# A perceiver block on one core: token groups cut as 2, 4, 4, 4, 2 batches in place of 4, 4, 4, 4

## What is computed

```python
x = x + cross_attention(_layernorm(x), ctx)      # q, k, v.reshape(B, -1, 16, 64): 16 heads over pairs of rows, softmax
x = x + selective_scan_block(_layernorm(x))      # 1024 channels, 16 states
x = x + moe_ffn(_layernorm(x))                   # 16 experts, the best 4 of a token, 512 -> 256 -> 512
```

```python
x_inner = x @ x_proj_w.T;  xc = silu(causal_conv4(x_inner) + conv_b)
B = x @ B_proj_w.T;  C = x @ C_proj_w.T
delta = softplus(x @ dt_proj_w.T + dt_proj_b);  A = -exp(A_log)
h = exp(delta * A) * h + delta * B * xc          # a recurrence over the 64 tokens of a batch
y = sum_s(h * C) + D * xc;  out = y @ out_proj_w.T
```

## Time and profile before

| | |
|---|---|
| median of 3 runs | 1436.08 us (1433.49 to 1438.27) |
| profiled execution | 1434.95 us, its span 1432.4 us |
| TensorE busy | 1084.5 us (76%) |
| VectorE busy | 990.2 us (69%) |
| ScalarE busy | 610.1 us (43%) |
| chain that ended last | VectorE 41%, TensorE 38%, ScalarE 8%, DMA 8% |
| granted TensorE clock, mean | 0.87 |

### The profile page before, as it was taken

The page is one execution under the profiler, slowest core; times in us unless marked ns, Lnnn a source line. Parts: engine busy times, 40 slices in busy tenths (PEclk is TensorE's granted clock), DMA queues, the critical chain, the costliest instruction groups (busy, mean ns, idle before and its releaser), DMA issues.

```text
span 1432.4 us, 12665 instructions
## 1 busy us (share of the span) xinstructions
PE 1084.5 (76%) x3996; PEld 698.7 (49%) x3996; DVE 990.2 (69%) x934; ACT 610.1 (43%) x1350; POOL 127.2 (9%) x113
## 2 busy tenths in 40 slices
PE   6997756777685588597578669437787799999993
PEld 4775634555454456474356547313343344545451
DVE  1201599879989999988999997857686785414312
ACT  4441573345275455355545526413443332222221
POOL 0010002211000060000014000030000000223102
PEclk9998986788898798799789779568999899999997
DMA  7355006999300253230035230085898796899994
GB/s 261 103 177 226 10 15 236 400 349 342 133 8 15 66 154 109 57 131 7 15 103 158 55 133 15 15 282 199 263 302 292 256 297 233 303 371 406 410 402 122
DMA packets 114033, 266.15 MB, mean 186 GB/s; under 512 B 10160, under 2 KB 43056, under 8 KB 113968
## 3 DMA queue, kind: packets, MB, share of 16 engines
q1 hardware_dynamic: 98096, 207.16, 42.6%
q0 software_dynamic: 15872, 58.20, 10.4%
HBM read 197.03 MB, written 68.29 MB: 185 GB/s over the span
## 4 chain that ended last, share of the span: by engine, by line
DVE 41%; PE 38%; ACT 8%; DMA 8%; issue 3%; POOL 1%; SPq 0%; POOLq 0%; DVEq 0%; ACTq 0%
DVE state L1244 14%; PE bank L745 13%; DVE state L1241 7%; PE bank L713 6%; DVE y_acc L1251 6%; DVE state L1247 5%; PE bank L766 5%; ACT decay L998 4%; PE bank L640 3%; PE bank L663 3%; DMA queries_ctx<-in_dt_t 2%; DMA ctx<-in_ctx_t 2%; DMA bc_bcast<-bc_scratch 2%; PE bank L735 1%; PE bank L641 1%
## 5 line engine op out<-in xcount | busy, mean ns | idle before, releaser
L1244 DVE TENSOR_TENSOR_SCAN state<-decay,state 128x2048 f32<-128x2048 f32 x64 | 282.9, 4420 | 13.0 <-ACT decay L998 12.0
L745 PE MATMUL bank<-expert_w,block_x_t 128*128 128x512 f32 x496 | 243.7, 638 | 43.5 <-ACT block_x_t L1048 43.5
L640 PE MATMUL bank<-ctx,queries_ctx 128*128 128x256 f32 x512 | 156.6, 460 | 46.4 <-ACT queries_ctx L887 23.3
L745 PEld LDWEIGHTS bank<-expert_w,block_x_t 128*128 128x128 f32 x496 | 96.7, 205 | 147.4 <-issue 101.1
L1388 DVE SCALAR_TENSOR_TENSOR hidden<-hidden,bank 128x256 f32<-128x256 f32 x62 | 26.1, 421 | 193.2 <-ACT hidden L1052 187.6
L998 ACT ACTIVATE decay<-delta_odd,params 128x256 f32<-128x256 f32 x256 | 106.3, 497 | 118.5 <-DVE state L1244 109.0
L640 PEld LDWEIGHTS bank<-ctx,queries_ctx 128*128 128x128 f32 x512 | 112.2, 230 | 80.7 <-ACT queries_ctx L887 25.4
L663 PE MATMUL bank<-probs,ctx 128*128 128x256 f32 x512 | 135.4, 424 | 18.8 <-ACT probs L922 14.4
L1251 DVE TENSOR_TENSOR y_acc<-y_acc,state 128x2048 f32<-128x2048 f32 x64 | 146.6, 2291 | 1.9
L1247 DVE TENSOR_TENSOR state<-state,bc_bcast 128x2048 f32<-128x2048 f32 x64 | 146.2, 2284 | 1.1
L1534 POOL DMA_INDIRECT dispatched<-ffn_x,slot x32 | 65.6, 2051 | 852.8 <-DVE slot L1333 844.2
(11 more groups left out here) (184 smaller groups left out, 1279.8 us busy)
## 6 DMA issues: line engine op xcount, KB each, us to landing
dispatched<-ffn_x POOLq DMA_DIRECT2D x38, 1024.0 KB, 20.9
expert_w<-in_eg_t SPq DMA_DIRECT2D x62, 512.0 KB
expert_w<-in_eu_t SPq DMA_DIRECT2D x62, 512.0 KB
expert_w<-in_ed_t SPq DMA_DIRECT2D x62, 512.0 KB
ctx<-in_ctx_t SPq DMA_DIRECT2D x32, 512.0 KB, 6.8
ctx<-in_ctx_n SPq DMA_DIRECT2D x32, 512.0 KB, 3.7
bc_bcast<-bc_scratch SPq DMA_DIRECT2D x64, 256.0 KB, 5.3
block_x<-dispatched SPq DMA_DIRECT2D x62, 256.0 KB
```

Of the source, the lines that this page charges most:

```text
L640: pe.matmul(o, QT[g][:, k, c, qb * P:(qb + 1) * P], ctxT[n % 2][:, c, :], start=(c == 0), stop=False)
L745: mm = pe.matmul(o, xbT[q % 2][:, c, :], w_gu[q % NW][:, :, c, :], start=(c == 0), stop=(c == DC - 1))
L1244: dve.tensor_tensor_scan(h, dA[n % 2][:, 0:sw], h, 0.0, ALU.mult, ALU.add).then_inc(scan_rd, 1)
```

## The change

- `GBS` becomes (2, 4, 4, 4, 2): five groups, of which the first and the last are one tile of 128 tokens and four attention units. There are four loops of attention beside scans instead of three. The first expert wave is still the first three groups, now five tiles and 35 blocks; the second is groups 3 and 4, three tiles and 27 blocks.
- Routing and table of the first wave stand inside loop 3. Beside its half attention only ten of group 3's steps stand (`UNIT_STATES`, `TAIL`, `PRE`).
- The other six steps of group 3 and all sixteen half-width steps of group 4 are spread over all 35 blocks by weight (`scan_work`). ScalarE and SyncE take the entries of step j-1 in step j. Group 4's sum goes to a buffer of its own (`y_acc_last`).
- Group 3's output product is in step 14, its routing follows in steps 15 to 20. Group 4's output product, routing, slots, the second table and dispatch stand between the waves, and the second wave's weights are loaded after its table.
- The key bias is spread by ScalarE, eight activations in place of one VectorE pass.
- Clears of the first wave's buffer (24 pieces) are paced over scores 1 to 11, those of the second (16 pieces, copied from zero rows in memory) over scores 14 to 21.
- The transposed block and the down product have one bank each in place of two.

```diff
-GBS = (4, 4, 4, 4)
+GBS = (2, 4, 4, 4, 2)
-WAVES = ((0, 1, 2), (3,))
+WAVES = ((0, 1, 2), (3, 4))
-CLEAR_UNITS = range(8, 16)
+CLEAR_UNITS = [range(1, UNIT0[2]), range(UNIT0[2] + 2, UNIT0[3] + 2)]
-LEAD, TAIL, PRE = 4, 2, 2
+LEAD = 4
+UNIT_STATES = [NS - 8] * (NGR - 2) + [4]
+TAIL = [2] * (NGR - 2) + [1]
+PRE = [2] * (NGR - 2) + [1]
+LATE = LEAD + UNIT_STATES[-1] + TAIL[-1] + PRE[-1]
+def scan_work():
+
+    n0, n1 = (NGR - 2) * NS + LATE, NGR * NS
+    todo = [(n, p, GBS[n // NS] * (2 if p == 1 else 1)) for n in range(n0, n1) for p in range(SCAN_PARTS)]
+    total = sum(v for _, _, v in todo)
+    out = {j: [] for j in range(-1, BLOCKS[0])}
+    gone = 0
+    for n, p, v in todo:
+        out[gone * (BLOCKS[0] + 1) // total - 1].append((n, p))
+        gone += v
+    return out
...
+            for j in range(NW):
+                load_gate_up(0, j)
+                load_down(0, j)
+            store_bc(NGR - 1)
+            for t in range(TAIL[-1], TAIL[-1] + PRE[-1]):
+                load_bc((NGR - 2) * NS + LEAD + UNIT_STATES[-1] + t + 2)
+            sp.wait_ge(dl_rdy, NGR)
+            for j in range(NX):
+                load_block_x(0, j)
...
-                        for state, part in scan_parts(j - 1):
-                            if part == SCAN_PARTS - 1 and state + 2 < NS:
-                                load_bc((NGR - 1) * NS + state + 2)
+                        for k, part in SCAN_WORK.get(j - 1, []):
+                            if part == SCAN_PARTS - 1 and k + 2 < NGR * NS:
+                                load_bc(k + 2)
...
-                    mm = pe.transpose(bank[q % 2][:, c * P:(c + 1) * P], v[:, c, :], ident)
+                    mm = pe.transpose(bank[0][:, c * P:(c + 1) * P], v[:, c, :], ident)
...
-            ffn_logits(NGR - 2)
-            positions(NGR - 2)
+            pe.wait_ge(d_free, jd.n)
             experts(0)
+            out_proj(NGR - 1)
+            ffn_logits(NGR - 1)
+            positions(NGR - 1)
             experts(1)
...
+            def key_bias(g):
+
+                b = job_a()
+                if g:
+                    act.wait_ge(bc_out, 16 * g)
+                for h in range(H):
+                    ins = act.activation(sb8[g][:, :, h, :], b[0:H, 0:GTS[g]].rearrange("p (u i) -> p u i", u=NUS[g]),
+                                         ACT.Copy, scale=ident[0:H, h:h + 1])
...
-                        for state, part in scan_parts(j):
-                            if part == 1 and state + 2 < NS:
-                                scan_decay(NGR - 1, state + 2)
+                        for k, part in SCAN_WORK.get(j - 1, []):
+                            if part == 1 and k + 2 < NGR * NS:
+                                scan_decay((k + 2) // NS, (k + 2) % NS)
...
+            pool.wait_ge(zero_rdy, 1)
+            clear(0)
+            dispatch(0)
+            clear(1)
+            for c in range(1, NGR):
                 dispatch(c)
```

200 lines of the change are left out of this document (89 added, 111 removed).

## The result

The changed kernel takes 1473.38 us (median of four runs, 1472.2 to 1474.4), against 1435.61 us for the kernel before, run beside it: a ratio of 1.0255, with a 95% interval from 1.0221 to 1.029. The forecast was 1435 us, no change, in a range of 1406 to 1463. The kernel is some 38 us slower, outside the range. The profiled execution has a span of 1470.8 us, against the forecast sum of 1432.7, so 38 us have to be found.

The account below looks back on a forecast made before the run. VectorE was taken to bound the loops, TensorE the blocks from 1165 us. Start of wave one 946.5 + wave one 237 + gap 58.5 + wave two 155.4 + tail 35.3 = 1432.7, with 2.5 around it 1435 us; range 1406 to 1463.

Parts of the forecast that it names:

- The clears: Clears spread over eleven attention units: nothing beyond the ends above, at some 370 GB/s; 2 us for the second batch.
- stage 0 and loop 0: First group's attention, 117 us after 178; then four-batch attention beside two-batch scans, 184 us, bounds 174 to 200.
- Loops 1 and 2 at 471: Still bound by VectorE: 477.9 us less two key biases of 2.3 and about 4 for one tile, plus 2 for clears.
- Rival (c): Clears hold up context loads: each of eleven units loses 2.9 us, result 32 later, 1467 us; chance 0.08.
- Wave one, 237: First expert wave, 35 blocks: 224 us at TensorE's pace, plus 5 for routing and 8 for late B and C loads.
- The mechanism "second": In wave one SyncE issues the B and C load behind the block's weights: 8 us, bounds 0 and 28.
- Rival (b): Half-width scan steps bind wave one through late B and C loads: 19 us more, gap 5, total 1459; chance 0.18.
- Between the waves, 58.5: In series: scan lag 13, output product 8, normalising 3, logits 4, routing 9, table 4, then 17.5 to first product.
- the handover: From the last scan inputs to wave one's first gate/up product: block load and transpose only, 5.5 us instead of 58.5.
- wave two: Second expert wave, 27 blocks for 23: 131.3 us plus 4 times 5.86, and 0.7 for a low-starting clock: 155.4.
- over 6.2 us a block only if VectorE waits for B and C: Sign for wave one: block period 5.86 us up to its middle, over 6.2 after it only with such waits.
- Wrong if loop 0 is near 240: Sign that the forecast is wrong: loop 0, put at 184 us, still takes near 240.

Follow-up runs that it names:

- the run with four buffers: Changed kernel with four buffers for the last group's B and C rows, each loaded two states further ahead: 1465.68 us, ratio 1.0155 to the kernel before.
- the wave with 29 steps: The split kernel at ratio 0.9804 with wave one's scans spread over 29 of its steps, not 32: 1418.22 us, ratio 0.9865 to the kernel before.
- the 32 steps: Split kernel with the three faults mended, wave one's scans spread over 32 of its steps, not 36: 1425.63 us, ratio 0.9907 to the kernel before.

## Where the prediction failed, step by step

**The clears.** This is the step that failed most: "I put them at nothing beyond the ends above", and for the second batch "plus 2". The first batch was weighed by its rate over eleven units. The second was not looked at beyond its size. Two things could have been read before. The diff gives the second batch another source, memory, which no row of before shows, so it had no price and should have had bounds of its own. And the clears wait on GpSimd behind the scatters of group 0, so thresholds 14 to 16 are passed when it comes to them: a wait for a count paces nothing once the engine arrives late. The second batch cost 13.3 us (251.7 against 238.4).

**Luck in stage 0 and loop 0.** The first batch was put at nothing too, and it cost 2.9 us in stage 0 (112.7 against 109.8) and about 10 in loop 0 (187.6 and 188.3 against 177.6). The two stages together still met the forecast, 300.3 us against 301. That is luck: without the clears they take 287.5, so the rest of their sum was 13 us too long, as much as the clears cost. Which of its terms were too long, the runs do not separate. The forecast also read VectorE as busy 224 of 238 us "in the three loops"; in loop 0 of the kernel before it was 211 of 240.

**Loops 1 and 2 at 471.** Without the copies they take 238.4 + 238.6, 477.0 us; the remaining 5 us of loop 1's miss are here. I subtracted VectorE's saved work from the loop as if VectorE filled it. VectorE is busy 218.1 of 238.5 us in the mended loop 1, in the old one 224.5 of 238.2: 6 us less work, no less time. The key bias alone did pay, between 2 and 5 us a loop; why the saved routing did not, no run shows.

**Rival (c)** had the right cause and half of the place: it charged 2.9 us to every unit of the first batch, 32 us in all, where that batch costs some 13, and as much again came from the second, on which it had nothing. The sentence on the Trainium skill ("DMA: Bandwidth & Descriptors", "Queues, rings and completion order") belonged to it: each DMA engine alternates between queue rows by packets. The runs agree in part: from packets of 23 KB on the clears' queue to 3.8 KB with the same source, VectorE's longest wait for B and C fell from 19.5 to 4.2 us and the natural-layout context landed after 10.8 us in place of 29.3, but the transposed context after 22.5 in place of 11.6. Whether the packets that the profile counts are those of this rule, no run shows. That clears in flight delay the loads, however small their packets, agrees too (8.2 to 13.8 us even with the on-chip source, against 6.1 in the earlier trace rows); but whether a delay costs time depends on what stands beside it: in the old kernel with its clears moved, loop 1 carried 27 of them, up to 1 MB each, and was 0.8 us longer.

**Wave one, 237.** The mechanism "second" (the B and C load issued behind the block's weights) was right, and it was priced at 8 us with 28 as its upper bound. It measures 13.5 us in the wave and 3.8 in the gap, 17.3. The landing, taken from the earlier trace rows as 7.7, was 11.2 in the median: those rows come from a wave whose DMA engines were 79% busy at 259 GB/s, and in the second part of the mended one they are 86% busy at 306. Without the late loads the wave takes 233.7, where the sum would have had 229; what the other 5 us are, no run takes apart. Rival (b) named this mechanism, with 24 us.

**Between the waves, 58.5.** The lag of the scans (forecast 13, measured 14.2), the product (8, 8.8) and the stretch from there to the table (20, 17.8 from 1238.87 to 1256.66) were about right. The term that failed is the last one: from the table to the first product 17.5 us were put where 25.2 were taken (1256.66 to 1281.82). I had named the queue behind 4.7 MB of weights, and still scaled the old 22.1 us down for half the scatters. The four scatters were all issued by 1258.5, the rows were asked for at 1267.24 and landed 11.8 us later, and the run with the rows among the weights shows that this order costs 6.5 us.

**What was right.** Loops 2 and 3, the handover, wave two and the tail came within 3 us each. (The 0.7 us of wave two "for a clock that starts low" has no row behind it; the granted clock of that wave is 0.99.) With the three faults mended the split kernel takes 1434.2 us, the forecast's "no change", with the luck above in it. Of the signs named to look for, "over 6.2 us a block only if VectorE waits for B and C" was seen in part: TensorE's period was 8.4 to 10.9 us at such waits (from 1142.08 and 1188.54), but also 11.5 us at the routing of group 3 (from 1081.59), and the run with four buffers has that one too. "Wrong if loop 0 is near 240" was a poor sign, for it did not watch the loop where the new kind of transfer ran.

**What stays open.** How much of the copy's harm is packet size and how much is reading memory (7.8 and 5.5 us from one trace each), and whether it matters that all copies read the same 512 rows; why SyncE's issue was held for 12.62 us; what sets the clock of a run, on which loop 0 hangs by 11 us; what lengthens the wave with 29 steps.

With the clears mended in both, the split into five groups is worth 0.9804 (0.9779 to 0.9829) against 0.9847 (0.9822 to 0.9873), some 6 us with intervals that still touch, and it needs the four buffers, the order of loads and the 32 steps for it. Most of what was to be won lay in the clears of the old kernel.
